# Feature crossing on one Trainium2 core: turned steps take the later stage as the stationary operand, with a new order of steps

## The reference

```python
z = jnp.sum(x, axis=-1)
xi = x[:, II, :]
xj = x[:, JJ, :]
outer = jnp.einsum('bpd,pde,bpe->bp', xi, kernels, xj)
h = jnp.concatenate([z, outer, dense_ctx], axis=1)
h = jnp.maximum(h @ W_top1 + b_top1, 0.0)
h = jnp.maximum(h @ W_top2 + b_top2, 0.0)
y = h @ W_top3
```

## Time and profile before

| | before |
|---|---|
| median of 3 runs | 815.76 us (815.51 to 815.84) |
| the profiled execution | 816.48 us |
| its span | 814.7 us |
| PE busy | 768.5 us (94%) |
| DVE busy | 722.7 us (89%) |
| ACT busy | 682.0 us (84%) |
| POOL busy | 607.1 us (75%) |

### The profile page before, as it was taken

How to read it: one execution, slowest core, us unless ns; L and a number is a source line. 1 busy time by engine, 2 the same in 40 slices (tenths; PEclk the granted TensorE clock), 3 DMA queues, 4 the chain that set the end, 5 groups by cost and what they waited for, 6 DMA issues and landing times.

```text
span 814.7 us, 20371 instructions
## 1 busy us (share of the span) xinstructions
PE 768.5 (94%) x6000; PEld 451.0 (55%) x6000; DVE 722.7 (89%) x684; ACT 682.0 (84%) x5282; POOL 607.1 (75%) x966
## 2 busy tenths in 40 slices
PE   0389989999999999999999999999999999999998
PEld 0245445565655655565556556555565656565556
DVE  0269999989999899989999899999999899998992
ACT  1049897899879997899888998799978998889983
POOL 6776888888888887888868887888868888682000
PEclk9889999999999999999999999999999999999999
DMA  4545111111111111111111111111111111110000
GB/s 135 162 148 166 27 26 24 26 24 26 25 27 25 24 26 21 27 25 24 26 20 24 26 23 23 25 24 26 24 21 25 25 25 26 20 25 8 1 2 1
DMA packets 20014, 28.74 MB, mean 35 GB/s; under 512 B 9024, under 2 KB 9664, under 8 KB 19008
## 3 DMA queue, kind: packets, MB, share of 16 engines
q0 software_dynamic: 16384, 16.81, 10.7%
q1 hardware_dynamic: 3520, 10.63, 3.9%
HBM read 27.40 MB, written 0.01 MB: 34 GB/s over the span
## 4 chain that ended last, share of the span: by engine, by line
PE 79%; POOL 8%; DMA 6%; issue 3%; DVE 2%; ACT 1%; DVEq 0%; POOLq 0%
PE m_ps L649 24%; PE m_ps L633 24%; PE acc L663 13%; PE tr L572 8%; POOL gathered L310 7%; DMA gathered<-in_tbl,idx 6%; PE tr L553 4%; PE tr L586 3%; PE m_ps L572 1%; DVE prod L475 1%; POOL x_half L293 1%; ACT turned_act L409 1%; PE m_ps L635 1%; DVE turned_act L500 1%; PE tr L567 0%
## 5 line engine op out<-in xcount | busy, mean ns | idle before, releaser
L409 ACT ACTIVATE turned_act<-turned_act 128x64 f32<-128x64 f32 x2560 | 611.9, 244 | 2.7 <-DVE turned_act L500 2.6
L310 POOL DMA_INDIRECT gathered<-in_tbl,idx x512 | 489.4, 956 | 101.1 <-issue 76.6
L409 ACT ACTIVATION_READ_ACCUMULATOR turned_act<-turned_act 128x1 f32 x2560 | 488.3, 191 | 0.0
L475 DVE TENSOR_TENSOR prod<-m_ps,x_t 128x1024 f32<-128x1024 f32 x256 | 307.5, 1214 | 21.2 <-PE m_ps L635 20.3
L633 PE MATMUL m_ps<-x_t,k_sb 64*128 64x256 f32 x1024 | 269.1, 389 | 4.2 <-DVE turned_dve L500 2.6
L635 PE MATMUL m_ps<-x_t,k_sb 64*128 64x256 f32 x1024 | 269.4, 390 | 0.0
L649 PE MATMUL m_ps<-k_sb,x_t 64*128 64x512 f32 x1024 | 257.1, 609 | 1.3 <-DVE turned_dve L500 0.7
L633 PEld LDWEIGHTS m_ps<-x_t,k_sb 64*128 64x128 f32 x1024 | 184.4, 188 | 112.4 <-issue 73.7
L500 DVE TENSOR_TENSOR turned_act<-m_ps,gathered 128x1024 f32<-128x1024 f32 x160 | 192.5, 1215 | 13.9 <-PE m_ps L649 6.0
L635 PEld LDWEIGHTS m_ps<-x_t,k_sb 64*128 64x128 f32 x1024 | 184.2, 188 | 0.0
L293 POOL TENSOR_TENSOR x_half<-gathered 128x32 f32<-128x32 f32 x448 | 117.1, 262 | 30.0 <-DVE z_nat L459 20.8
(11 more groups left out here) (36 smaller groups left out, 152.8 us busy)
## 6 DMA issues: line engine op xcount, KB each, us to landing
gathered<-in_tbl,idx POOLq DMA_INDIRECT x512, 2.5
k_sb<-in_kmat SPq DMA_DIRECT2D x7, 1024.0 KB, 4.9
w_sb<-in_w SPq DMA_DIRECT2D x1, 1280.0 KB, 9.0
k_sb<-in_kmat SPq DMA_DIRECT2D x2, 256.0 KB, 3.2
k_sb<-in_kmat SPq DMA_DIRECT2D x1, 512.0 KB, 5.0
w_sb<-in_w SPq DMA_DIRECT2D x1, 512.0 KB, 10.9
idx<-in_ids SPq DMA_DIRECT2D x1, 256.0 KB, 2.7
z_sb<-in_dense_t SPq DMA_DIRECT2D x8, 16.0 KB, 1.8
```

The source lines that it names most:

```text
L310: nc.gpsimd.indirect_dma_start(out=gathered[:, t, G % GR, f * D:(f + 1) * D], out_offset=None, in_=tables[2 * (STAGES - 1 - a) + f], in_of ...
L409: last = nc.scalar.activation(row, row, ACT.Copy, accum_out=z_turned[:, q % 2, t, 16 * c + n:16 * c + n + 1])
L475: nc.vector.tensor_tensor(prod[:, r % PR, :, :].rearrange("p u (e n) -> p u e n", e=2), m_ps[:, p % MR, :, :].rearrange("p u (e n) -> p u ...
```

## The change

Three quarters of the turned entries now pair an earlier block with a later stage: (0, 4..7), (1, 8..11) and (2, 12..15); the entries (2, 0..3) stay. The pairs of stages covered are other ones, their number is the same, and the even steps take the rest. There are again 32 even and 32 turned steps of the same shapes, 12 turned ones summed by DVE. The order, the places of all other jobs, which turned steps DVE sums and where, and the places of the transposes in round 0 (`FIRST_AHEAD`) are new. Blocks 0, 1 and 2 now have turned steps, the last of them in a later round with index 14, 44 and 61.

```diff
-TURNED = [(1, _m) for _m in range(4)] + [(2, _m) for _m in range(4)] + [(3, _m) for _m in range(8)]
+TURNED = [(0, 4), (0, 5), (0, 6), (0, 7), (1, 8), (1, 9), (1, 10), (2, 0), (2, 1), (2, 2), (2, 3), (1, 11),
+          (2, 12), (2, 13), (2, 14), (2, 15)]
-BY_VECTOR = [_i in (1, 5, 6, 10, 12, 16, 18, 21, 23, 26, 28, 30) for _i in range(NT)]
+BY_VECTOR = [_i in (3, 5, 6, 7, 10, 15, 17, 19, 21, 25, 29, 31) for _i in range(NT)]
-        if (_a // COLS, _m) not in TURNED:
+        if (_a // COLS, _m) not in TURNED and (_m // COLS, _a) not in TURNED:
-TURNED_FIRST = [3, 3, 5, 7, 7, 7, 9, 10, 11, 12, 15, 16, 17, 18, 18, 19, 19, 19, 19, 21, 21, 22, 24, 25, 25, 26,
-                27, 28, 29, 29, 31, 31]
-TURNED_LATER = [0, 1, 3, 5, 5, 7, 8, 8, 9, 11, 11, 11, 12, 12, 14, 14, 15, 16, 16, 17, 17, 20, 21, 22, 22, 24, 24,
-                26, 28, 28, 29, 29]
+TURNED_FIRST = [1, 2, 2, 2, 3, 4, 4, 5, 5, 6, 6, 6, 7, 8, 10, 10, 10, 11, 11, 12, 13, 14, 16, 17, 18, 20, 20, 23,
+                26, 26, 27, 29]
+TURNED_LATER = [0, 1, 1, 2, 4, 5, 6, 6, 7, 8, 9, 9, 10, 11, 11, 13, 15, 15, 17, 17, 17, 18, 18, 20, 21, 22, 23, 25,
+                26, 27, 28, 29]
...
-    ("x", 0, BEHIND, -3, 1),
-    ("x", 2, AHEAD, -1, -1),
-    ("x", 4, BEHIND, -1, 2),
-    ("x", 6, BEHIND, 1, 0),
-    ("x", 8, BEHIND, 5, 1),
-    ("x", 10, BEHIND, 11, 1),
-    ("x", 12, BEHIND, 15, 1),
-    ("x", 14, BEHIND, 21, 3),
-    ("xsum", 0, AHEAD, -3, 0),
-    ("t", 0, BEHIND, 3, 0),
-    ("h1", 0, BEHIND, 9, 2),
-    ("h1", 1, AHEAD, 12, 1),
-    ("h1", 2, AHEAD, 14, 2),
-    ("h1", 3, BEHIND, 17, 0),
-    ("h2", 0, AHEAD, 24, 1),
-    ("h2", 1, AHEAD, 26, 0),
-    ("y", 0, AHEAD, 28, 2),
+    ("x", 0, BEHIND, -11, 2),
+    ("x", 2, BEHIND, -7, -1),
+    ("x", 4, AHEAD, -4, -1),
+    ("x", 6, AHEAD, 2, 1),
+    ("x", 8, AHEAD, 6, -1),
+    ("x", 10, BEHIND, 7, 4),
+    ("x", 12, BEHIND, 11, 1),
+    ("x", 14, BEHIND, 17, 0),
+    ("xsum", 0, BEHIND, -3, 1),
+    ("t", 0, BEHIND, 1, 0),
+    ("h1", 0, AHEAD, 4, -1),
+    ("h1", 1, AHEAD, 7, 1),
+    ("h1", 2, BEHIND, 9, 4),
+    ("h1", 3, BEHIND, 15, -1),
+    ("h2", 0, AHEAD, 18, 2),
+    ("h2", 1, BEHIND, 19, 1),
+    ("y", 0, BEHIND, 23, 0),
 )
-KEEP_Z_LATER = 0
+
+FIRST_AHEAD = (0, 0, 0, 1, 1, 2, 3, 4, 5, 6, 7, 8, 11, 12, 15, 16)
+KEEP_Z_LATER = -1
...
-    AHEAD.setdefault((0, max(0, FIRST[_a] - 1)), []).append(("x", 0, _a))
+    AHEAD.setdefault((0, FIRST_AHEAD[_a]), []).append(("x", 0, _a))
...
-VECTOR_SUMS_BEHIND = (1, 3, 5, 6, 7, 8, 9, 12, 13, 16, 17, 22, 25, 31)
+VECTOR_SUMS_BEHIND = (0, 2, 3, 9, 13, 15, 17, 19, 22, 23, 24, 26, 31)
```

## The result

The changed kernel takes 823.06 us (median of 6 runs, 822.68 to 823.79), the kernel before 815.81 in the same comparison. The ratio is 1.0086, with a 95% interval of 1.0076 to 1.0096: 0.9% slower. The profiled execution took 822.99 us, with a span of 821.2. The page of the changed kernel: busy time by engine, then the chain by engine.

The account below looks back on a forecast made before the run. PE bounds the later rounds, with POOL's stream limiting what round 0 gains. -1.3 + 7 x 0.6 + 0.3 = +3.2, less 0.3 for the last round: +2.9 on 816.5 gives 819.4, median 818.7 us; range 813 to 824.

Parts of the forecast that it names:

- Step 5: POOL's gathers of stages 8 to 11 wait for T31: 0 to 0.8 us a round, 0.3 taken for all; x4 just met.
- third rival: The hold on block 2 or ACT's lateness costs every round, 1.19 us each: +7.1 in six rounds, 825.8 us; chance 0.19.
- Step 2: Order of a later round on PE: 21 blocks of steps instead of 19, +0.6 us a round, +4.2 for seven rounds.
- The rival built on the Trainium skill: Blocks of steps on PE cost nothing more: -1.0, 814.8 us, no measurable change; chance 0.12.
- Step 3: Round 0: DVE gets 4 instructions ahead, 4.5 us; PE reaches X4 at about 121, POOL has it ready at 125.9.
- second rival: POOL's first 67 gathers run faster because loads of matrices collide less with them: 815.3 us; chance 0.16.
- Step 4: From X4 on: dense start of round 1 at 134.4 against 135.7 before, with 0.8 for DVE's late restart; gain 1.3.
- Steps 1, 6, 7: Turned entries' equal work, ACT's lateness, and SP, stores and the end: nothing saved or added, the last within 0.5.

Follow-up runs that it names:

- ring: The changed kernel with 20 places for gathered stages instead of 16 and 7 for products instead of 8: 814.21 us, on a chip without pauses.
- shorter halving: The changed kernel with each halving on POOL adding one number of each piece instead of 32: 813.65 us.
- E9: Not a run: an even step on PE, last of a block of steps in a later round of the changed kernel that takes 3.67 us.
- E11: Not a run: an even step on PE, last of a block of steps in a later round of the changed kernel that takes 4.71 us.
- fewer blocks: The changed kernel with T31 and T23 one even step earlier and x4, x8, xsum next to a reduce, 19 blocks instead of 21: 813.75 us.
- E0: Not a run: the even step on PE that is the start of a round.

## Why the prediction was right or wrong

The sign and the range were right and the mechanism of the holds was named with its two places. The size was not: +7.25 us against +2.9. Three terms of the sum were mis-sized, and two of the errors went against the third. That the time lies inside the stated range is in part luck: with the error of step 5 alone put right, the sum would have been 818.7 + 8.3 = 827.0, outside it.

- **Step 5, the hold on POOL: the step that failed.** It took 0.3 us for all rounds; the runs give 8.6, by two ways with the same period of 94.71 (ring, shorter halving), and a third way (T31 and T23 moved) took all the waits away as well, at 94.94. The prediction's bounds for T31's product were 1.7 before the round's start and the start itself, and it took the near one. Two things make it the far one. The sum of T29 stands in front of T31's product on DVE, since there is one buffer for these; the prediction counted 0.96 of matmuls and 1.13 of DVE and nothing between. And from a product's end to the gather it releases there are 0.8 us, which it did not count at all. With both, stage 8's gather starts at 516.34 and the round at 516.32. The distances were right: PE would have been at x10 25.7 behind the start, and POOL needs 26.4. For T23 the 0.8 would only have used up the forecast's slack: product out 24.6 before the next round, PE at x4 8.5 before it, so 16.1 us between them, where POOL needs 0.8 + 15.3. But PE came to x4 at 603.41, only 15.5 behind the product's end at 587.90, and "just met" became 0.56. That this stretch of PE was 0.6 shorter than forecast fits step 2, whose surcharges were too dear; it was not followed block by block. The forecast's bound of 0.8 was kept for x10 only; x4's wait was given no price and cost 0.56 of the 1.28 us.
- **The third rival** was this mechanism, with 1.19 us a round as its price (measured: 1.43) and "0.3 us more lag of DVE at T31" as its point. Measured, T31's product ended at 515.55 and not at 512.53 + 0.96 + 1.13 = 514.62, 0.9 late, 0.8 of it behind the sum of T29. Its total of 825.8 was too high only because it rested on steps 2 and 4.
- **Step 2, the order on PE**: forecast +0.6 us a round, measured +0.135 for the same 21 blocks. The second surcharge is not a constant: T8 E8 T9 E9 takes 547.02 - 543.35 = 3.67 in the changed kernel, where the round-0 block of the earlier trace rows took 3.85; T10 T11 E10 T12 E11 takes 555.08 - 550.37 = 4.71, 0.41 more than 5 x 0.86. And two blocks cost 0.32 between the runs with and without *fewer blocks* and 0.135 here, so if blocks are all that differs, the price of one is between 0.07 and 0.16, not 0.20, as one reads it from whole rounds. Two surcharges read from single blocks were multiplied by counts, without a check on a whole round of before. The rival built on the Trainium skill ("TensorE: Matmul & The Clock Gate", Part 3, The mechanism: a weight load is pulled ahead of running matmuls if it goes to other row groups or to the background weight buffer) says 0, nearer to the measured 0.135 than 0.6 is, but not met: the run with fewer blocks gained 0.32 by them alone. Whether weight loads are what a block pays for was not tested.
- **Step 3, round 0**: right in kind. DVE's busy time from 34 to 50 is 11.17 us; in the same stretch before it was 3.16:

```profile
34.00:50.00 16.00, 7.96 (x39) 3.47 (x38) 3.16 (x5) 1.15 (x3) 11.77 (x13) 0.57 0.49 156
```

But PE came to X4 at 123.35 and not at 121, and POOL had it at 124.4 and not at 125.9, so the wait was 1.07 and not 4 to 5. POOL's first halving came at 91.99 and not at 93.47: of the second rival (POOL's first 67 gathers faster, by up to 5.2 us as it was priced, 88.8 - 83.1 = 5.7 by its own rows) 1.5 came true. What made them faster was not tested.
- **Step 4, the start of round 1**: forecast a gain of 1.3, measured 3.1. From X4 to E0 it is 132.04 - 124.42 = 7.62, as forecast (7.7). 1.5 of the difference are POOL's. The rest is that the 0.8 for DVE's restart was not paid: from E0 to x10 of round 1 PE stands only once, 0.46 at x10, and that is for POOL.
- **Steps 1, 6, 7**: nothing, as forecast. Busy sums are equal, PE waits for no product of ACT in a later round, and the end is 16.4 us in both.

Put together: 818.7 - 1.8 (step 4) - 3.3 (step 2) + 8.3 (step 5) = 821.9. Of the 1.1 left 0.7 is that the profiled execution of before lay that far above its median and the one of after does not.

Left open: what makes the engines pause on some chips; the ring in the kernel before, and ring with fewer blocks, on a chip without pauses; x4's place alone; why POOL's first gathers gained 1.5 us.

## What to carry to other kernels

When an edit changes who reads a ring buffer last, follow the release to its end: the producer engine's queue in front of the releasing instruction (a forced sum in a single buffer here), the time from its end to the waiting issue, and then the consumer's pace up to the place where the bound engine needs it. "Just met" is a wait as soon as one of these is left out, and it is paid in each round. Give each such place a price of its own, and set a surcharge that was read from one block against a whole round before you multiply it by a count.

## What the runs showed of the hardware

From the end of a DVE product to the POOL gather that it releases there are 0.79 and 0.80 us, the same in both places. PE's granted clock from 34 to 50 us, a mean of its two levels of 1.2 and 2.4 GHz, rose from 0.57 to 0.89 with the denser steps of round 0: before, PE was busy for 7.96 of these 16 us and stood mostly for gathers otherwise, after, for 13.82. And chips differ: on some the kernel before took 1221 to 1241 us and not 815.9, with PE's mean clock at 0.83; in the traces taken there DVE's instructions last as long as elsewhere, and engines stand for long stretches for a releaser that the profile doesn't name, while POOL can go on. There the new order with the ring was 5.5 to 5.7% faster than the kernel before, but the old order with the ring 0.5 to 0.7% slower. The cause of the pauses was not found.
